# Two elementwise pieces of a convolution's front move from VectorE to ScalarE, and some signals are merged

## The reference, cut to what matters

```
h = _layernorm(x, axis=-1) * (1 + ca) + sa
proj = h @ W_in
raw, gate = split(proj)                  # 512 features each
conv = causal depthwise convolution of raw over tokens, 4 taps
h = silu(conv + conv_b)
ts, Bmat, C = split(h @ W_x)
dt = softplus(ts @ W_dt + b_dt);  A = -exp(A_log)
state[t] = exp(dt[t] * A) * state[t-1] + dt[t] * Bmat[t] * h[t]     # 16 states a feature
y = (sum over states of state * C + h * D) * silu(gate)
x = x + ga * (y @ W_out)
```

## Time and profile before

| | us |
|---|---|
| median of 3 runs (lowest to highest) | 2576.57 (2573.95 to 2578.89) |
| the profiled execution, and its span | 2574.13, 2572.4 |
| TensorE busy | 2278.5 (89%) |
| VectorE busy | 1738.1 (68%) |
| ScalarE busy | 1373.4 (53%) |
| GpSimd busy | 1336.6 (52%) |

### The profile page before, as it was taken

The page is one execution under the profiler, slowest core; times in us unless marked ns, Lnnn a source line. Parts: engine busy times, 40 slices in busy tenths (PEclk is TensorE's granted clock), DMA queues, the critical chain, the costliest instruction groups (busy, mean ns, idle before and its releaser), DMA issues.

```text
span 2572.4 us, 27213 instructions
## 1 busy us (share of the span) xinstructions
PE 2278.5 (89%) x8580; PEld 1485.1 (58%) x8580; DVE 1738.1 (68%) x2794; ACT 1373.4 (53%) x1816; POOL 1336.6 (52%) x1152
## 2 busy tenths in 40 slices
PE   4798999989999986688998998998998998998978
PEld 1466766667667552245655654654655655665667
DVE  4345455555554559898798798688688689688730
ACT  1243443525435363466766766766766766765622
POOL 2143252332523235566766756666666666657733
PEclk7899999999999997898999998998999998999989
DMA  6145555564445464445645645645545545546623
GB/s 231 33 137 177 178 161 161 168 199 136 141 137 160 159 204 124 125 132 151 173 131 152 172 132 146 167 138 144 164 136 153 168 134 140 163 136 170 187 69 97
DMA packets 253774, 384.79 MB, mean 150 GB/s; under 512 B 19168, under 2 KB 159984, under 8 KB 253632
## 3 DMA queue, kind: packets, MB, share of 16 engines
q1 hardware_dynamic: 223408, 281.33, 38.1%
q0 software_dynamic: 30224, 101.73, 12.8%
HBM read 345.93 MB, written 47.55 MB: 153 GB/s over the span
## 4 chain that ended last, share of the span: by engine, by line
PE 58%; DVE 15%; issue 11%; ACT 8%; POOL 6%; DMA 2%; DVEq 0%; SPq 0%; POOLq 0%; ACTq 0%
PE bank L233 25%; PE bank L239 8%; PE bank L1555 8%; PE bank L240 8%; DVE w_st L1485 3%; DVE bank L1477 3%; POOL d_in L1467 3%; PE bank L1080 2%; DVE cv L1295 1%; PE bank L1757 1%; PE bank L737 1%; PE bank L739 1%; PE bank L738 1%; PE bank L1758 1%; POOL f1L L1633 1%
## 5 line engine op out<-in xcount | busy, mean ns | idle before, releaser
L1467 POOL TENSOR_TENSOR d_in<-u,bc 128x512 f32<-128x512 f32 x512 | 658.8, 1296 | 365.0 <-DMA bc<-bc_rows 293.7
L1477 DVE TENSOR_TENSOR_SCAN bank<-bank,d_in 128x512 f32<-128x512 f32 x512 | 626.0, 1223 | 95.9 <-ACT bank L1533 62.9
L1555 PE MATMUL bank<-w_st,ident 128*128 128x512 f32 x1024 | 538.4, 640 | 85.0 <-DVE w_st L1485 84.8
L1533 ACT ACTIVATE bank<-dt,a_neg 128x512 f32<-128x512 f32 x512 | 348.2, 689 | 436.5 <-DVE w_st L1485 434.9
L1485 DVE TENSOR_TENSOR w_st<-bank,bc 128x512 f32<-128x512 f32 x512 | 345.2, 674 | 124.8 <-PE bank L1555 124.7
L239 PE MATMUL bank<-f1H,w_ring 128*128 128x512 f32 x768 | 357.3, 465 | 50.9 <-ACT raw L1364 21.5
L1555 PEld LDWEIGHTS bank<-w_st,ident 128*128 128x128 f32 x1024 | 196.5, 201 | 301.9 <-DVE w_st L1485 170.4
L240 PE MATMUL bank<-f1L,w_ring 128*128 128x512 f32 x768 | 308.7, 402 | 0.0
L239 PE MATMUL bank<-f0H,w_ring 128*128 128x512 f32 x512 | 230.8, 451 | 3.6 <-POOL f0L L1633 3.6
L1633 POOL TENSOR_TENSOR f0L<-mid,f0H 128x512 fp32r<-128x512 f32 x128 | 170.1, 1330 | 108.8 <-DVE f0H L1661 77.5
L239 PEld LDWEIGHTS bank<-f1H,w_ring 128*128 128x128 f32 x768 | 149.6, 195 | 128.2 <-issue 78.0
(11 more groups left out here) (210 smaller groups left out, 3966.6 us busy)
## 6 DMA issues: line engine op xcount, KB each, us to landing
bc<-bc_rows SPq DMA_DIRECT2D x256, 512.0 KB, 5.1
w_ring<-w_units POOLq DMA_DIRECT2D x160, 512.0 KB, 4.2
w_exp<-L_ffn_ew SPq DMA_DIRECT2D x240, 256.0 KB, 4.5
eo_rows<-eo SPq DMA_DIRECT2D x56, 256.0 KB, 4.2
xs<-xs_rows SPq DMA_DIRECT2D x24, 512.0 KB, 4.2
w_units<-h_T SPq DMA_DIRECT2D x16, 512.0 KB
xA<-L_attn_x SPq DMA_DIRECT2D x8, 512.0 KB, 6.0
x_mid<-xA SPq DMA_DIRECT2D x8, 512.0 KB
```

What stands on the lines that cost most here:

```text
L1467: pool.tensor_tensor(d_in[:, nth(b, s) % IN, :], u[:, c, :], rows_tile(b, use)[:, 0, :], ALU.mult).then_inc(in_made.sem, 1)
L1477: dve.tensor_tensor_scan(bank[:, :], bank[:, :], d_in[:, nth(b, s) % IN, :], 0.0, ALU.mult, ALU.add).then_inc(scanned.sem, 1)
L1533: act.activation(state_bank(b, s)[:, :], dt[:, c, :], ACT.Exp, scale=a_neg[:, c, n:n + 1]).then_inc(dA_made.sem, 1)
L1555: pe.matmul(y_bank(c)[:, :], ident[:, :], w_st[:, nth(b, s) % WG, :], start=False, stop=(n == NST - 1)).then_inc(summed.sem, 1)
```

## The change

The first tap that is made for a tile is now the one without a shift (the newest token): ScalarE makes it, as a Copy scaled per partition, right after its copy to `raw`, and VectorE adds the other three with multiply-adds. The norm of the front is applied by ScalarE as an Identity with scale rstd and bias -mean * rstd, for which VectorE makes a small 128x4 tile `minus_mean`. In both layers pairs of signals that one chain increments in turn become one signal with twice the count.

```diff
-PLAN = dict(
+PLAN = dict(xhat_act=34.8,
...
-            q_scaled, q_made = signal("q_scaled", TT), signal("q_made", TT)
-            k_scaled, k_made = signal("k_scaled", TT), signal("k_made", TT)
+            q_step, k_step = signal("q_step", 2 * TT), signal("k_step", 2 * TT)
...
-                    dve.wait_ge(*q_scaled.at(b, t + 1))
-                    dve.tensor_tensor(q_tok[:, t, :], q_tok[:, t, :], os_rows[:, 0, 1, :], ALU.add).then_inc(q_made.sem, 1)
+                    dve.wait_ge(*q_step.at(b, t + 1))
+                    dve.tensor_tensor(q_tok[:, t, :], q_tok[:, t, :], os_rows[:, 0, 1, :], ALU.add).then_inc(q_step.sem, 1)
...
@@ front_sync
-                    sp.wait_ge(*normB.step.all(b - 1))
+                    sp.wait_ge(*xhat_made.all(b - 1))
@@ front_vector
                 yield F + PLAN["norm_apply"]
                 if b:
-                    dve.wait_ge(*h_made.all(b - 1))
-                norm_apply(normB, b, xB, xhatB)
+                    dve.wait_ge(*xhat_made.all(b - 1))
+                dve.wait_ge(*normB.rstd_made.all(b))
+                dve.scalar_tensor_tensor(out=minus_mean[:, :], in0=normB.stat[:, :, 0], scalar=-1.0, in1=normB.rstd[:, :], op0=ALU.mult,
+                                         op1=ALU.mult).then_inc(normB.step.sem, 1)
                 for c in range(KI):
                     o, r = cv[:, c % 2, :], raw[:, c % 2, :]
                     yield F + PLAN["conv"] + PLAN["raw_gap"] * c
-                    dve.wait_ge(*raw_made.at(b, c + 1))
-                    if c == 0:
-                        dve.wait_ge(*b_turned.all(b))
-                        if b == 0:
-                            dve.wait_ge(*pad_made.all(0))
-                    if c >= 2:
-                        dve.wait_ge(*h_made.at(b, c - 1))
-                    dve.tensor_scalar(o, r[:, 0:S], conv_w[:, 0, c:c + 1], None, ALU.mult).then_inc(tap_made.sem, 1)
-                    for tap in range(1, KC):
-                        yield F + PLAN["conv"] + PLAN["raw_gap"] * c + PLAN["tap_gap"] * tap
-                        dve.wait_ge(*tap_made.at(b, c * KC + tap))
+                    if b == 0 and c == 0:
+                        dve.wait_ge(*pad_made.all(0))
+                    for tap in range(TAPS):
+                        yield F + PLAN["conv"] + PLAN["raw_gap"] * c + PLAN["tap_gap"] * (tap + 1)
+                        if tap:
+                            dve.wait_ge(*tap_made.at(b, c * TAPS + tap))
+                        else:
+                            dve.wait_ge(*last_tap.at(b, c + 1))
                         dve.scalar_tensor_tensor(out=o, in0=r[:, tap:tap + S], scalar=conv_w[:, tap, c:c + 1], in1=o,
                                                  op0=ALU.mult, op1=ALU.add).then_inc(tap_made.sem, 1)
@@ front_scalar
+                yield F + PLAN["xhat_act"]
+                act.wait_ge(*normB.step.all(b))
+                if b:
+                    act.wait_ge(*dt_made.all(b - 1))
+                for t in range(TT):
+                    i = act.activation(xhatB[:, t, :], xB[:, t, :], ACT.Identity, bias=minus_mean[:, t:t + 1], scale=normB.rstd[:, t:t + 1])
+                i.then_inc(xhat_made.sem, 1)
                 for k in range(KD):
                     yield F + PLAN["hT_act"] + k
...
                     act.activation(raw[:, c % 2, PAD:], shared.bank["raw", b, c][:, :], ACT.Copy).then_inc(raw_made.sem, 1)
+                    act.wait_ge(*raw_made.at(b, c + 1))
+                    if c == 0:
+                        act.wait_ge(*b_turned.all(b))
+                    act.activation(cv[:, c % 2, :], raw[:, c % 2, PAD:], ACT.Copy, scale=conv_w[:, TAPS, c:c + 1]).then_inc(last_tap.sem, 1)
@@ front_tensor
                 yield F + PLAN["turn"]
-                pe.wait_ge(*normB.step.all(b))
+                pe.wait_ge(*xhat_made.all(b))
```

More of the change, by code:

```diff
@@ L344, in adaln_kernel @@
             qk_done, qk_biased, qk_act = signal("qk_done", TT), signal("qk_biased", TT), signal("qk_act", TT)
[L345 to L346 removed]
+            q_step, k_step = signal("q_step", 2 * TT), signal("k_step", 2 * TT)
             hid_done, hid_act = signal("hid_done", 2 * KH), signal("hid_act", 2 * KH)
[L348 removed]
+            sim_done, sim_max, sim_exp = signal("sim_done", KH), signal("sim_max", 2 * KH), signal("sim_exp", KH)
             asum_step, gated = signal("asum_step", 2), signal("gated", KH)
@@ L464, in setup_scalar @@
                 act.wait_ge(*c_in.all(0))
-                act.activation(c_act[:, :, :], c_tok[:, :, :], ACT.Silu).then_inc(c_act_made.sem, 1)
+                act.activation(c_act[:, :, :], c_tok[:, :, :], ACT.Silu).then_inc(c_step.sem, 1)
                 act.wait_ge(hid_weights_in.sem, 2 * 16)
@@ L470, in setup_tensor @@
                 pe.wait_ge(consts_made.sem, 2)
-                pe.wait_ge(*c_act_made.all(0))
+                pe.wait_ge(*c_step.at(0, 1))
                 for l in range(2):
@@ L476, in setup_tensor @@
                 i.then_inc(modT_turned.sem, 1)
-                pe.wait_ge(*cT_made.all(0))
+                pe.wait_ge(*c_step.all(0))
                 for l in range(2):
@@ L536, in decay_rates_scalar @@
                 act.wait_ge(a_log_in.sem, 16)
-                act.activation(a_neg[:, :, :], a_neg[:, :, :], ACT.Exp).then_inc(a_exped.sem, 1)
+                act.activation(a_neg[:, :, :], a_neg[:, :, :], ACT.Exp).then_inc(a_step.sem, 1)
             def decay_rates_vector():
                 yield x1_at(1) + PLAN_A["rates"] + 2
-                dve.wait_ge(*a_exped.all(0))
-                dve.tensor_scalar(a_neg[:, :, :], a_neg[:, :, :], -1.0, None, ALU.mult).then_inc(a_made.sem, 1)
+                dve.wait_ge(*a_step.at(0, 1))
+                dve.tensor_scalar(a_neg[:, :, :], a_neg[:, :, :], -1.0, None, ALU.mult).then_inc(a_step.sem, 1)
                 dve.wait_ge(ssm_weights_in.sem, 5 * 16)
@@ L743, in att_tensor @@
                     if d == 0:
-                        pe.wait_ge(*q_made.all(b))
-                        pe.wait_ge(*k_made.all(b))
+                        pe.wait_ge(*q_step.all(b))
+                        pe.wait_ge(*k_step.all(b))
                     products(tile(14 + d)[:, :], lambda t: q_tok[:, t, d * P:(d + 1) * P], lambda t: k_tok[:, t, :], TT
@@ L1527, in core_scalar @@
                         if b == 0 and s == 0:
-                            act.wait_ge(*a_made.all(0))
+                            act.wait_ge(*a_step.all(0))
                             act.wait_ge(*s2_out.all(B - 1))
```

33 lines of the change are left out of this document (18 added, 15 removed).

## The result

| | before | after |
|---|---|---|
| median of 20 runs (lowest to highest), us | 2579.63 (2573.95 to 2585.07) | 2573.79 (2565.09 to 2579.66) |
| ratio of the two, 95% interval | | 0.9976 (0.9968 to 0.9985) |
| the profiled execution, and its span, us | 2574.13, 2572.4 | 2572.19, 2570.5 |

The time, 2573.8 us, lies inside the range that was given (2556 to 2602), but on the other side of before than the forecast of 2584: some 6 us less in place of 7.5 more. What follows therefore takes sizes of whole kernels from the ratios, and from the traces the lengths of stretches that repeat.

The account below looks back on a forecast made before the run. VectorE was taken to bound the front, TensorE the remainder. Fronts 2 to 7 gave +9.0, front 1 -2, front 0 +0.5: +7.5 us, so 2584 from the 2576.57 median; 8-in-10 range 2556 to 2602.

Parts of the forecast that it names:

- Merged signals: Both layers: each merged pair is incremented by one engine in the old order, waiters wait for the same instruction; 0.
- Norm, fronts 2 to 7: ScalarE's Identities wait for the small instruction and push table loads, Silus, decay 14 and scan 14 back: +3.1 us a front.
- +0.8 and +0.5 for fronts 1 and 0: The norm's turn comes later: +0.8 us in front 1, which with its taps was taken as -2, and +0.5 in front 0.
- Tile 0: Fronts 2 to 7: VectorE gains the first tap, 0.54 us in two fronts, 2.63 in four where GpSimd's products held it.
- Tile 1: Fronts 2 to 7: 0.5 us saved, but VectorE soon waits for TensorE and ScalarE's next decays come 0.78 later; -0.2.
- Tile 2: Fronts 2 to 7: the Copy delays table load and decays, so the scan comes 0.5 us later instead of 0.4 earlier; +0.5.
- rival (c): The next tap with both inputs in SBUF takes over the hold, five long taps give 0.5: 2595 us or above; chance 0.17.
- Tile 3 and the rest: Fronts 2 to 7: tile 3 lies where TensorE bounds, and the remainder stays unchanged; 0.
- (a): VectorE's relief passes through, decay 14 isn't on the path, the Identities lie beside other work: -22, 2554 us; chance 0.20.
- (b): Engines in the front are coupled so closely that losses and gains vanish in TensorE's order: 2577 us; chance 0.15.
- (d): The added ScalarE functions need their own table, two more loads in each front: +18, 2602 us; chance 0.03.
- the three signs of being wrong: Scan 14 within about 4.5 us of weigh 11; tables loaded ahead of the Identities; tile 0's first STT becoming 2.6 us.

Follow-up runs that it names:

- Norm alone: The whole change with all four taps back on VectorE, so merged signals and the norm on ScalarE: 2598.79 us, ratio 1.0058 to the kernel before.
- taps alone: The whole change with the norm back on VectorE, so merged signals and the unshifted tap on ScalarE: 2560.71 against 2581.04 us, ratio 0.9915 to the kernel before.
- the three traces: Profiled executions of the kernel before, of the same kernel once more (2582.57 us), and of the kernel with only merged signals (2581.72 us, ratio 0.9996).
- signals alone: Only the merged signals of the change, norm and all four taps on VectorE: 2581.72 against 2581.04 us, ratio 0.9996 to the kernel before.
- the Copy dropped: Merged signals, norm and three taps on VectorE, unshifted tap left out of the computation, no ScalarE Copy: 2555.76 against 2586.57 us, ratio 0.9874 to the kernel before.

## Why the forecast had the wrong sign

**Merged signals: 0.** Right (0.9996).

**Norm, fronts 2 to 7: +3.1 us each, 18.6.** The mechanism is shown: the Identities behind `minus_mean`, the load behind them, decay 14 late, scan 14 late by 3.17 us six times; and making the Identities start without their wait took 1.24 off. The four took 2.08 us against the 1.9 that I worked out. The rule of the Trainium skill, ScalarE: Activation LUTs, section "What ACT_TABLE_LOAD costs", gave 2.06, and the trace agrees with it. What didn't hold is that all of the delay lasts: by step 16 it is 2.7 (14.09 less 11.38), six times 16.2. Norm alone measured +16, with 8 either way, where this term with +0.8 and +0.5 for fronts 1 and 0 had promised +19.9. It is a term of the right kind, by the trace 0.4 us a front too dear, and by the times not wrong.

**Tile 0: -0.54 with a short tap, -2.63 with a held one.** On average -1.93, and the stretch measured -1.94. The hold did not pass on there: after, the first tap of tile 0 took 0.73 in all six fronts. Front 7:

```profile
2125.56 0.73 DVE L1297 SCALAR_TENSOR_TENSOR cv<-raw,conv_w,cv 128x512 f32<-128x512 f32 x1
```

**Tile 1: -0.2.** Here the size was wrong: -0.74 in the change and -0.54 in taps alone. VectorE's wait for TensorE in front 7 is 1.69 us where it was 1.70, so it didn't take the saved tap as I had it, and no scan of tile 1 waits for a decay in either trace.

**Tile 2: +0.5.** This number came out near (+0.69 in the change) by luck. The chain is there as worked out, with Copy, table load, two decays and a scan behind them:

```profile
2150.08 0.72 ACT L1378 ACTIVATE cv<-raw,conv_w 128x512 f32<-128x512 f32 x1
2150.82 1.28 ACT L1547 ACT_TABLE_LOAD   x1
2152.11 1.30 ACT L1547 ACTIVATE bank<-dt,a_neg 128x512 f32<-128x512 f32 x2
```

The scan at 2152.90 waited 0.91 us for it. But this front's tile 2 is no longer than before (10.99 us), nor are those of fronts 2 and 6, and in taps alone, where the same wait of 0.91 stands, the stretch was even (-0.08). What the Copy's chain costs at this scan doesn't last to the end of the tile. The mean of +0.69 is that of three fronts at nothing and three at some +1.5, which have the held second tap shown above. That the hold moves on was rival (c), and not this term.

**Tile 3 and the rest: 0.** +0.11 and -1.04 against the mean of the three traces; those three reach from 119.45 to 120.59 in the rest, so a gain there can't be told from scatter. Over all fourteen traces the rest takes 119.5 us in the nine kernels with fewer taps on VectorE (118.55 to 120.25) and 120.1 in the five with all four (119.45 to 120.59): 0.6 us less, a hint and no more, as the two groups overlap. Front 1: from the first scan to step 12 of core 1, 206.8 us in taps alone against 209.6 in the mean of the three, -2.8, the -2.8 that the taps were given there; in the whole change 208.4, -1.2 against the forecast's -2.

**The step that failed** is the sum of the taps: what their move frees on VectorE, less what the Copies cost, was put too low. By the prediction's own terms the taps gave -9.8 in fronts 2 to 7 (-1.93, -0.2 and +0.5, six times) and -2.8 in front 1, together -12.6. Measured alone they gave -21 beside signals alone, and 15 to 29 us less than before, which leaves -12.6 just outside. Two of the terms are mis-sized in the trace of taps alone as well: tile 1 by 0.3 us a front (0.5 in the change), and tile 2 by 0.6, where a charge of +0.5 met a stretch that stayed even. A third, the held tap of tile 0, was priced by its own length (2.1 us more than a short one), while fronts that have one are 2.8 us longer over the whole period; how much of that leaves with the tap isn't shown.

For the whole change, whose interval is narrow (2 us either way), all terms together were about 13 us too high (+7.5 against -6). Its trace places ten of them, as differences to the prediction over fronts 2 to 7: norm 6 x 0.4 = 2.4, tile 1 6 x 0.54 = 3.2, tiles 2 and 3 back by 6 x 0.3 = 1.8, and the rest 6 x 1.04 = 6.2, the largest entry and the least sure, for the reason above. The others aren't placed. Nor does the trace of taps alone hold the whole of their gain: its fronts 2 to 7 are shorter by 11.0 us and front 1 by 2.8, together 14 of 21. That execution (2563.6 us) was the slowest of its five, and those that it is compared with were partly fast ones. The forecast took "the remainder unchanged"; whether a remainder of TensorE's work shortens when the front before it delivers earlier wasn't tried by itself, and stays open.

A part of it is the ground of the sum. The profiled execution of before took 2574.1 us and the three runs shown had a median of 2576.6; the median of 20 is 2579.6. The four held taps that I counted were one sample of a number that was three, four and five in three traces, at 2.1 us each, so two traces alike in code differ by that alone.

**The rivals.** (a), *VectorE's relief passes through*, priced the taps that VectorE sheds at 21 us and took 7 off for the Copies at tile 2, so 14 against the 12.6 that I had let pass. Taps alone gave 21, and with no Copies at all (the Copy dropped) 31, so both sums were too low, (a)'s a little less. For the norm (a) was wrong, since decay 14 and scan 14 were level as the prediction said, and its total of -22 is far from -6. (b), *TensorE holds the end*, falls: single parts moved the time by 16 and 21 us. It has a grain of truth in VectorE's waits from 1130 to 2500 us (waiter, releaser, us, times, longest), before and after:

```profile
DVE w_st L1485 <- PE bank L1555: 122.8, 61, 5.4
```

```profile
DVE w_st L1499 <- PE bank L1569: 133.0, 64, 5.4
```

With VectorE's work 32 us shorter, its waits for TensorE's sums grew by 10. (c), *the hold moves on*: the mean of the taps hardly changed (1064 ns against 1071) since the 3.1 us tap of tile 1 stayed, and in fronts 3 to 5 a tap of tile 2 became a 2.3 us one, at some 1.5 us a front. So it is true in part; but the five long taps of tile 0 that this rival asked for didn't come. (d), *more table loads*: 341 loads before and after, 123 of them ahead of a decay in both; it falls.

With two opposite terms of about 20 us each, an error of a fifth in one and two fifths in the other was larger than their difference. The chances said as much (0.25 for faster); the forecast's sign rested on less than its terms' bounds. That the time lies inside the range is owed to the range's width, which took in most of rival (a), and not to the sum. None of the three signs of being wrong came either: scan 14 starts 7.5 us after weigh 11, the tables are loaded behind the Identities, and the first tap of tile 0 is a short one. They all watched the norm and tile 0, and the error lay behind them.

## What to carry to other kernels

When a change moves work between two in-order engines, its time is the small difference of a relief and a delay: price each, and then measure each by itself, since the sum tells neither. Look in a group of instructions for its longest, not at its mean: each of two taps among sixteen, which took 2.6 and 3.1 us for 0.5 and 0.7 us of work, gave some 10 us when it was issued about a step later, where the whole change gave 6. Then look where the hold went, for here one turned up at tile 2, in three fronts of the change and in all six when the tap of tile 1 was moved. And take the ground of a sum from several executions, for one profile of the kernel before can stand 5 us from its median and hold events that come and go.

## What the runs showed of the hardware

**VectorE held by GpSimd.** A product of SBUF data on VectorE (the TENSOR_SCALAR and the multiply-add of the taps) that starts while a product of GpSimd runs, or 0.04 us ahead of it, ends only after it: 2133.38 + 3.10 = 2136.48, 0.55 us after the end of two products at 2135.93; the TENSOR_SCALAR of 2130.50 ends at 2133.15, 0.30 after 2132.85. In these two cases it waits for two products, although they are separate instructions. It need not be so. In the kernel before, front 7, tile 3, VectorE and GpSimd:

```profile
2169.57 1.67 DVE L1295 SCALAR_TENSOR_TENSOR cv<-raw,conv_w,cv 128x512 f32<-128x512 f32 x1
```

```profile
2168.20 2.49 POOL L1633 TENSOR_TENSOR f1L<-mid,f1H 128x512 fp32r<-128x512 f32 x2 [0.36 <-ACT f1H L1706]
2170.65 3.17 POOL L1467 TENSOR_TENSOR d_in<-u,bc 128x512 f32<-128x512 f32 x2
```

The tap ends at 2171.24, 0.55 us after the product that was under way when it started, and the next pair of products, right behind, takes 3.17 us in place of 2.54: now GpSimd waits for VectorE. A scan and a weigh with an operand in PSUM keep their time beside such products (1.21 and 0.67 us). Nor does GpSimd come first always. In the changed kernel a GpSimd product that started 0.16 us after a tap took 1.74 in place of 1.28 us:

```profile
2129.26 0.74 DVE L1297 SCALAR_TENSOR_TENSOR cv<-raw,conv_w,cv 128x512 f32<-128x512 f32 x1
```

```profile
2129.42 1.74 POOL L1647 TENSOR_TENSOR f0L<-mid,f0H 128x512 fp32r<-128x512 f32 x1 [1.43 <-DVE f0H L1675]
```

The Trainium skill, SBUF — State Buffer, section "SBUF: two separate sides", describes the pair of ports that the two engines share as an exclusive lock, taken for the whole instruction by whichever starts first. The case of 2129.26 agrees, and so does that of tile 3. With the tap of 2133.38 VectorE's record starts 0.04 us ahead and it still waits for both products, so the record's start isn't the moment at which the lock is taken, or it changed hands in another way. No run here tells these apart.

**Table loads.** After a load of 1.28 us the next activation starts within 0.02 us (2111.39 + 1.28, then 2112.68), for 272 of the 341 loads of the kernel before; the others are followed by a longer gap, as where the activation waits for another engine.

**Scatter.** Twenty runs of one kernel spread over 11 to 15 us, 24 runs of the kernel before in another series over 25.5 (2567.3 to 2592.8), and the first scan started between 921.9 and 932.1 us in kernels whose first layer is the same.
